# The first block of a two-layer graph network on one Trainium2 core: order of the loads, a second pair of projection banks, and edge chunks turned one ahead

## Chip, cores, metric

The kernel runs on one core of one Trainium2 chip. The metric is the time of one execution on the device in microseconds (us), the median of several runs.

## What is computed

Two layers, each a graph convolution and a feed-forward part, over 6,250 nodes of 256 features and 100,000 edges sorted by destination. The change touches the start of the first convolution, an attention over edges (cut from the reference):

```python
ft = (feat @ W_fc).reshape(N, H, D)              # feat: layer norm of x; H = 8 heads, D = 32
eh = jnp.einsum('nhd,hd->nh', ft, attn_h)
et = jnp.einsum('nhd,hd->nh', ft, attn_t)
fe = (edge_attr @ W_e).reshape(-1, H, D)         # edge_attr: 100,000 x 64
ee = jnp.einsum('ehd,hd->eh', fe, attn_e)
e = jax.nn.leaky_relu(eh[src] + ee + et[dst], negative_slope=NEG_SLOPE)
```

After it come softmax and sum per destination, the first feed-forward part, a second convolution and 32 experts. None of these is changed.

## The kernel before

The program is a row of blocks: `front`, then the attention, the experts of layer 0, the second sums, and the rest. A block ends when all its engines have ended. `front` has five instruction streams written out by hand (SP, POOL, TensorE `pe`, ScalarE `act`, VectorE `dve`); each runs its own in order and meets the others only at semaphores. SP's stream is also the queue of all ordinary transfers.

**Projection.** x (125 partitions x 50 rows, in tile `GX`) comes in ten chunks of five rows (`load_x`, two transfers each). Rows are worked on two at a time, 25 groups: VectorE takes statistics (`stats`), ScalarE the root (`root`), VectorE the reciprocal (`spread`) and normalizes (`norm`); TensorE transposes the group into `pT` (`turn`, L580), ScalarE copies that to `xnT` (`copy_turned`, L655), TensorE multiplies by `Wext`, 272 columns (`project`, L591), ScalarE copies the result from its two PSUM banks `pF` into `row` and `ETS` (`rows`, L665 and L666), and SP stores `row` (`store`, L431). There are two `row` buffers, so the rows of group g wait for the store of group g-2. `project(g)` waits for `row_ready` g, the copies of the group before, since both use `pF`. In ScalarE's order the root of the chunk that group 5 needs stands behind `rows(2)`. Between the projections stand four pieces (`segments`, L572, with `segment_rows` on VectorE) that find where each node's edges begin; the last posts `ROWI` (L740), and POOL then gathers 51 columns of words (L522).

```python
for g in range(NGR):
    if 1 <= g <= len(SW):
        segments(g - 1)
    if g + 1 < NGR:
        turn(g + 1)
    project(g)
```

**Edges.** The edge attributes come in 49 chunks (`load`, three transfers of 512 KB in all, later two) into four buffers `ebuf`; the load of chunk c waits until chunk c-4 is turned. For a chunk TensorE makes eight transposes into `pE0` and `pE1` (`turn_edges`, L553), ScalarE copies both to `eT` (L638), TensorE multiplies by `VB` (`score`, L562, eight products that the profile counts as 16 passes), ScalarE keeps the result in `V` (L644).

```python
for c in range(NCH):
    turn_edges(c)
    ...
    score(c)
```

Into this loop come, at chunk 12, the prefix sum of `TOT` (L617), which VectorE makes from the gathered words (L836), at chunk 13 a second one, and at chunk 24 the turning of the edges' ranks. VectorE works on the ranks meanwhile; SP's queue carries them out and in between the edge loads of chunks 16 to 19 (L471 to L491), and the loads of chunk 19 on are issued behind them.

**POOL** scatters 50 columns of `ETS` (L532) after the words, and then gathers the first 64 columns of projected rows, 128 rows of 264 values each (L540), for the attention.

**End.** Behind the last edge load SP reads `F` (3,136 KB, L497). VectorE makes eight scans over it (L886), adds the scores (L891), SP stores them (L502), and the block ends.

## Time and profile before

| what | us |
|---|---|
| median of 3 runs (3243.67 to 3244.92) | 3244.02 |
| profiled execution, its own time | 3244.61 |
| span of the profile | 3242.9 |
| first block, up to the next one's first instruction | 369.7 |
| TensorE / POOL / VectorE / ScalarE busy over the span | 2347.0 / 1838.9 / 1756.4 / 1314.1 |

Times in the profile count from the start of the span. An engine's idle time stands in brackets ahead of an instruction, with what ended it. A row of the timeline merges neighbours of one kind (x8) and shows the time from the first's start to the last's end, so two merged rows of one engine can overlap by the pipeline's latency; where that matters, starts are compared with starts. "PEclk" is the granted clock of TensorE as a share of full speed (1.00 is 2.4 GHz, 0.50 is 1.2 GHz), "DMA share" the mean busy share of the 16 DMA engines.

### The profile page before, as it was taken

To read this page: it belongs to the slowest core of one execution; us is meant where nothing else is said; L and a number is where in the kernel's file an instruction comes from. 1 tells how busy PE (TensorE), PEld (TensorE's weight loads), DVE (VectorE), ACT (ScalarE), POOL (GpSimd) and SP (SyncE) were. 2 spreads that over 40 slices of the span, in tenths; PEclk is the share of its full clock that TensorE was granted. 3 is DMA by queue.
4 is the path that set the end of the run, shared out by engine and by line. 5 is a ranking of instruction groups with operands and counts; after the bars stand their busy time and mean duration, and the time that the engine had idled before them with its cause. 6 is when DMAs were issued, how large, how long until landed. Compare 5 with 4: busy or idle time off the path is not lost. (4 is left out here: it accounts for less than half of the span.)

```text
span 3242.9 us, 47998 instructions
## 1 busy us (share of the span) xinstructions
PE 2347.0 (72%) x11995; PEld 1955.5 (60%) x11995; DVE 1756.4 (54%) x5705; ACT 1314.1 (41%) x4659; POOL 1838.9 (57%) x1942
## 2 busy tenths in 40 slices
PE   4757476666676665577997888898788988646088
PEld 4656366666666565356776666676666766535077
DVE  5301688888888887466554433333333333366245
ACT  1323355555555444433444433333333332354033
POOL 2674377777777776131000777777777777250645
PEclk9989778888888877688998565655655566757589
DMA  6477444444444446540001333333333333321342
GB/s 194 119 169 202 141 113 112 112 112 113 111 113 112 112 112 156 182 119 23 26 14 43 106 106 106 106 105 105 106 106 106 106 106 105 113 59 28 103 143 85
DMA packets 266022, 349.58 MB, mean 108 GB/s; under 512 B 154605, under 2 KB 195475, under 8 KB 264245
## 3 DMA queue, kind: packets, MB, share of 16 engines
q0 software_dynamic: 89568, 235.89, 25.9%
q1 hardware_dynamic: 176190, 110.72, 13.4%
q8 instruction: 98, 1.61, 0.2%
q14 instruction: 166, 1.36, 0.1%
HBM read 289.49 MB, written 61.20 MB: 108 GB/s over the span
## 5 line engine op out<-in xcount | busy, mean ns | idle before, releaser
L1435 POOL DMA_INDIRECT Gb<-normed_rows,SRCT x784 | 741.2, 945 | 520.4 <-SPq L1427 281.9
L1456 PE MATMUL pAb<-HOTb,Gb 128*128 128x128 f32 x3136 | 843.7, 425 | 151.3 <-DMA Gb<-normed_rows,SRCT 118.1
L1456 PEld LDWEIGHTS pAb<-HOTb,Gb 128*128 128x128 f32 x3136 | 659.6, 297 | 335.5 <-DMA Gb<-normed_rows,SRCT 276.4
L1496 DVE TENSOR_TENSOR ACC<-ACC,pAb 128x256 f32 x784 | 330.7, 422 | 641.8 <-PE pAb L1456 568.6
L1026 POOL DMA_INDIRECT GX<-ft_rows,SRCT x432 | 412.6, 955 | 131.4 <-issue 129.6
L1115 ACT ACTIVATE ACC<-apA 128x254 f32 x784 | 301.0, 384 | 413.9 <-PE apA L1188 340.5
L1188 PE MATMUL apA<-AHOT,GX 128*128 128x129 f32 x1920 | 304.2, 328 | 83.0 <-DVE GX L1337 82.7
L1188 PEld LDWEIGHTS apA<-AHOT,GX 128*128 128x128 f32 x1920 | 289.2, 240 | 101.8 <-DVE GX L1337 101.7
L1475 ACT ACTIVATE HOTb<-OFFb 128x1024 f32<-128x1024 f32 x98 | 103.6, 1057 | 604.8 <-PE pAb L1456 604.6
L1026 POOL DMA_INDIRECT G<-ft_rows,SRCT x288 | 274.5, 953 | 87.6 <-issue 86.4
L1471 ACT ACTIVATE OFFb<-iota,NRELb 128x128 f32<-128x128 f32 x784 | 239.6, 388 | 6.7
L1188 PE MATMUL apA<-AHOT,G 128*128 128x129 f32 x1216 | 198.5, 335 | 48.1 <-DVE G L1337 46.1
L1188 PEld LDWEIGHTS apA<-AHOT,G 128*128 128x128 f32 x1216 | 189.2, 247 | 59.2 <-DVE G L1337 56.8
L1665 POOL DMA_INDIRECT Y<-sums_by_rank,RANKI x50 | 48.4, 968 | 169.9 <-POOLq L152 80.6
L1337 DVE TENSOR_TENSOR GX<-GX,apV 128x1024 f32<-128x1024 f32 x120 | 143.2, 1193 | 0.0
L562 PE MATMUL pS<-VB,eT 128*128 128x128 f32 x784 | 100.8, 283 | 50.3 <-ACT V L644 49.3
L1116 ACT ACTIVATE FL<-apA 128x4 f32<-128x4 f32 x784 | 134.5, 172 | 0.0
L562 PEld LDWEIGHTS pS<-VB,eT 128*128 128x128 f32 x784 | 92.8, 194 | 60.1 <-ACT eT L638 60.1
L2505 POOL DMA_INDIRECT out_dram<-sO,sID x80 | 77.8, 972 | 74.9 <-issue 42.1
L2253 POOL DMA_INDIRECT rows_by_expert<-PAY,POSI x50 | 49.6, 992 | 123.4 <-DVE POSI L2444 108.5
L1992 PE MATMUL fpM<-fxT,ffn_E 128*128 128x250 f32 x400 | 101.2, 407 | 25.2 <-ACT h L1920 25.2
L1237 DVE TENSOR_TENSOR AHOT<-apL,RELT 128x1024 f32<-128x1024 f32 x98 | 118.6, 1210 | 0.0
(390 smaller groups left out, 3968.0 us busy)
## 6 DMA issues: line engine op xcount, KB each, us to landing
ebuf<-in_edge_attr_dram SPq DMA_DIRECT2D x49, 448.0 KB
Gb<-normed_rows,SRCT POOLq DMA_INDIRECT x784, 2.7
rows_by_expert<-ffn_PADT SPq DMA_DIRECT2D x1, 10360.0 KB, 42.2
sT<-rows_by_expert SPq DMA_DIRECT2D x80, 129.5 KB, 2.2
GX<-ft_rows,SRCT POOLq DMA_INDIRECT x480
sums_by_rank<-rrowa SPq DMA_DIRECT2D x49, 128.0 KB, 1.7
sums_by_rank<-rrowb SPq DMA_DIRECT2D x49, 128.0 KB, 1.7
GX<-in_x_dram SPq DMA_DIRECT2D x11, 560.0 KB
```

Source lines behind the costliest of these rows:

```text
L562: last = nc.tensor.matmul(pS[:, m * 2 * H0:m * 2 * H0 + 128], eT[c % 2][:, m * EP:(m + 1) * EP], VB[:, :], start=True, stop=True)
L1026: pool.indirect_dma_start(G[c % GS][:, m, :], None, FT[:, :], bass.IndirectOffsetOnAxis(ap=SRCT[:, t:t + 1], axis=0)).then_inc(g_in[c % GS ...
L1115: nc.scalar.activation(acc[:, :, ds(r + 1, EP - 1)], sums[:, :, 1:EP], ACT.Copy)
L1116: nc.scalar.activation(FL[:, :, f:n + 1:n - f], sums[:, :, 0:HW:EP], ACT.Copy).then_inc(pfree[b], 1)
L1188: last = nc.tensor.matmul(pA[b][:, f * HW:(f + 1) * HW], G[c % GS][:, m, f * 128:(f + 1) * 128], HOT[c % 2][:, m, :], start=True, stop=True)
L1237: nc.vector.tensor_tensor(HOT[c % 2][:, h * HT:(h + 1) * HT, 0:EP], pL[0:EP, 256:256 + EP].unsqueeze(1).to_broadcast([EP, HT, EP]), RELT[: ...
L1337: nc.vector.tensor_tensor(v, v, pV[0:EP, 0:128].rearrange("p (h m) -> p h m", m=UT)[:, :, m:m + WB].rearrange("p h m -> p m h").unsqueeze( ...
L1435: pool.indirect_dma_start(G[g % R][m][:, :], None, TABLE[:, :], bass.IndirectOffsetOnAxis(ap=SRCT[:, t:t + 1], axis=0)).then_inc(g_in[g % ...
L1456: last = nc.tensor.matmul(pA[b][:, o:o + EP], G[k][m][:, c * 128:(c + 1) * 128], HOT[k % 2][:, m, :], start=True, stop=True)
L1471: nc.scalar.activation(OFF[k2][:, m, :], iota[0:EP, 0:EP], ACT.Abs, bias=NREL[k2][:, m:m + 1])
L1475: nc.scalar.activation(HOT[k2][:, :, :], OFF[k2][:, :, :], ACT.Relu, bias=1.0, scale=-1.0).then_inc(hot[k2], 1)
L1496: last = nc.vector.tensor_tensor(acc[:, :, ds(b, EP)], acc[:, :, ds(b, EP)], pA[q][:, o:o + KD * EP].rearrange("p (c r) -> p c r", c=KD), ...
```

## The change

Four things. On SP's queue x comes first: chunk 0 right behind the weights, chunk 1 behind the edge weights, chunks 2 to 9 behind the source indices; the padded destinations (`DXI`) move behind x, then the zeroes, then the four edge chunks; the row stores follow as before. The wait for `idx_set` moves behind chunk 0. The projection of group g uses `pF` for even g and `pE` for odd g (`pN`), and waits for the copies of group g-2. TensorE turns chunk c+1 ahead of the scores of chunk c; before chunk 0 it waits for `row_ready` 24, since `pE` is shared now.

```diff
--- before.py
+++ after.py
@@ -365,6 +365,7 @@
         pT = ps(s, "pT", [128, 512])
         pF = [ps(s, f"pF{m}", [128, 512]) for m in range(GT)]
         pE = [ps(s, f"pE{k}", [128, 512]) for k in range(2)]
+        pN = [pF, pE]
         pS = ps(s, "pS", [128, 512])
         pH = ps(s, "pH", [128, 512])
         pQ = ps(s, "pQ", [128, 512])
@@ -433,33 +434,32 @@
                 sp.dma_start(W[:, :, 0:D], W_fc.rearrange("(k p) n -> p k n", p=128)).then_inc(w_in, 16)
                 sp.dma_start(AH[:, :], attn_h.rearrange("h d -> (h d)").partition_broadcast(128)).then_inc(w_in, 16)
                 sp.dma_start(AT[:, :], attn_t.rearrange("h d -> (h d)").partition_broadcast(128)).then_inc(w_in, 16)
+                load_x(0)
+                ds32 = dst.rearrange("(p j) -> p j", j=BK * BW)
+                for a in PARTS:
+                    sp.dma_start(DVI[a, :], ds32[a, :]).then_inc(dv_in, 16)
                 sp.wait_ge(idx_set, 1)
+                sp.dma_start(SNI[0:P - 1, :], ds32[1:P, 0:1], allow_slow_non_contiguous=True).then_inc(dv_in, 16)
+                for k in range(2):
+                    sp.dma_start(WE[k * DE:(k + 1) * DE, :], W_e[:, :]).then_inc(we_in, 16)
+                sp.dma_start(AE[:, :], attn_e.rearrange("h d -> (h d)").partition_broadcast(128)).then_inc(we_in, 16)
+                load_x(1)
+                sp.dma_start(QI[:, 0:NB, :], src[0:NB * QB * EP].rearrange("(b q p) -> q b p", q=QB, p=EP)).then_inc(q_in, 16)
+                sp.dma_start(QI[0:QL, NB, :], sv).then_inc(q_in, 16)
+                sp.dma_start(QI[QL:QL + 1, NB, 0:E % EP], sl).then_inc(q_in, 16)
+                for q in range(2, NX):
+                    load_x(q)
                 sp.dma_start(DXI[0:112, 1:ES + 1], dv[0:112, :]).then_inc(ld, 16)
                 sp.dma_start(DXI[112:EF, 1:ES + 1], dv[112:EF, :]).then_inc(ld, 16)
                 sp.dma_start(DXI[EF:EP, 1:EL + 1], dl).then_inc(ld, 16)
                 sp.dma_start(DXI[1:EP, 0:1], dv[:, ES - 1:ES], allow_slow_non_contiguous=True).then_inc(ld, 16)
                 sp.dma_start(DXI[0:EF - 1, ES + 1:ES + 2], dv[1:EF, 0:1], allow_slow_non_contiguous=True).then_inc(ld, 16)
                 sp.dma_start(DXI[EF - 1:EF, ES + 1:ES + 2], dl[:, 0:1]).then_inc(ld, 16)
-                load_x(0)
-                ds32 = dst.rearrange("(p j) -> p j", j=BK * BW)
-                for a in PARTS:
-                    sp.dma_start(DVI[a, :], ds32[a, :]).then_inc(dv_in, 16)
-                sp.dma_start(SNI[0:P - 1, :], ds32[1:P, 0:1], allow_slow_non_contiguous=True).then_inc(dv_in, 16)
-                for k in range(2):
-                    sp.dma_start(WE[k * DE:(k + 1) * DE, :], W_e[:, :]).then_inc(we_in, 16)
-                sp.dma_start(AE[:, :], attn_e.rearrange("h d -> (h d)").partition_broadcast(128)).then_inc(we_in, 16)
-                sp.dma_start(QI[:, 0:NB, :], src[0:NB * QB * EP].rearrange("(b q p) -> q b p", q=QB, p=EP)).then_inc(q_in, 16)
-                sp.dma_start(QI[0:QL, NB, :], sv).then_inc(q_in, 16)
-                sp.dma_start(QI[QL:QL + 1, NB, 0:E % EP], sl).then_inc(q_in, 16)
-                load_x(1)
-                for c in range(ER):
-                    load(c)
-                    load_x(2 + c)
                 sp.wait_ge(v_zero, 1)
                 sp.dma_start(STARTD.rearrange("(p j) h -> p (j h)", j=ES), V[:, :]).then_inc(zero_in, 16)
                 sp.dma_start(RSUMD[RB * 128:RB * 128 + 1, :], V[0:1, 0:D]).then_inc(zero_in, 16)
-                for q in range(2 + ER, NX):
-                    load_x(q)
+                for c in range(ER):
+                    load(c)
                 for g in range(NGR):
                     store(g)
 
@@ -583,12 +583,12 @@
 
                 def project(g):
                     pe.wait_ge(xT_ready, g + 1)
-                    if g:
-                        pe.wait_ge(row_ready, g)
+                    if g >= 2:
+                        pe.wait_ge(row_ready, g - 1)
                     for m in range(GT):
                         for c in range(KD):
                             n = m * KD + c
-                            last = nc.tensor.matmul(pF[m][0:P, 0:WX], xnT[g % 2][:, n * P:(n + 1) * P], W[:, c, :],
+                            last = nc.tensor.matmul(pN[g % 2][m][0:P, 0:WX], xnT[g % 2][:, n * P:(n + 1) * P], W[:, c, :],
                                                     start=(c == 0), stop=(c == KD - 1))
                     last.then_inc(f_ready, 1)
 
@@ -610,8 +610,11 @@
                     project(g)
 
                 early, late = 3 * ER, 6 * ER
+                pe.wait_ge(row_ready, NGR - 1)
+                turn_edges(0)
                 for c in range(NCH):
-                    turn_edges(c)
+                    if c + 1 < NCH:
+                        turn_edges(c + 1)
                     if c == early:
                         pe.wait_ge(tot, 1)
                         nc.tensor.matmul(pQ[0:P, 64:65], below[0:P, 0:P], TOT[:, :], start=True, stop=True).then_inc(pre, 1)
@@ -662,8 +665,8 @@
                         act.wait_ge(stored[g % 2], 32 * (g // 2))
                     for m in range(GT):
                         i = g * GT + m
-                        nc.scalar.activation(row[g % 2][:, m, :], pF[m][0:P, 0:D + H0], ACT.Copy)
-                        last = nc.scalar.activation(ETS[0:P, i * H0:(i + 1) * H0], pF[m][0:P, D + H0:WX], ACT.Copy)
+                        nc.scalar.activation(row[g % 2][:, m, :], pN[g % 2][m][0:P, 0:D + H0], ACT.Copy)
+                        last = nc.scalar.activation(ETS[0:P, i * H0:(i + 1) * H0], pN[g % 2][m][0:P, D + H0:WX], ACT.Copy)
                     last.then_inc(row_ready, 1)
 
                 root(0)
```

On SP's queue, ahead of the stores, there stood before (the middle of the queue; names are tiles, `ebuf` an edge chunk, `GX` a chunk of x):

```order
L447 DMA SNI<-in_dst_dram 124x1
L449 DMA eT<-in_L_gnn_W_e_dram 64x256 x2
L450 DMA eT<-in_L_gnn_attn_e_dram 128x256
L451 DMA QI<-in_src_dram 112x6x128
L452 DMA QI<-in_src_dram 109x128
L453 DMA QI<-in_src_dram 1x32
L415 DMA GX<-in_x_dram 112x1280
L415 DMA GX<-in_x_dram 13x1280
L421 DMA ebuf<-in_edge_attr_dram 112x1024
L422 DMA ebuf<-in_edge_attr_dram 15x1024
L424 DMA ebuf<-in_edge_attr_dram 1x1024
L415 DMA GX<-in_x_dram 112x1280
```

Now the last of the queue ahead of the first edge chunk is:

```order
L457 DMA DXI<-in_dst_dram 1x1
L459 DMA et_at_starts<-V 128x6272
L460 DMA sums_by_rank<-V 1x256
L422 DMA ebuf<-in_edge_attr_dram 112x1024
L423 DMA ebuf<-in_edge_attr_dram 15x1024
L425 DMA ebuf<-in_edge_attr_dram 1x1024
```

and behind the fourth edge chunk come the first stores:

```order
L423 DMA ebuf<-in_edge_attr_dram 15x1024
L425 DMA ebuf<-in_edge_attr_dram 1x1024
L432 DMA ft_rows<-row 112x528
L432 DMA ft_rows<-row 13x528
```

All x chunks now lie ahead of `DXI`, zeroes and edges. The same transfers stand ahead of the first row store as before.

On TensorE, from the last two projections into the edge loop, there stood before (in brackets the semaphores that an instruction waits for; `attr_Tcopied` are ScalarE's copies of `pE`, `attr_in` the landed chunk):

```order
L591 MATMUL pF<-Wext,xnT 125x272 [waits row_ready,xT_ready]
L591 MATMUL pF<-Wext,xnT 125x272 x3
L591 MATMUL pF<-Wext,xnT 125x272 [waits row_ready,xT_ready]
L591 MATMUL pF<-Wext,xnT 125x272 x3
L553 MATMUL pE<-ident,ebuf 128x128 [waits attr_in0]
L553 MATMUL pE<-ident,ebuf 128x128 x7
L562 MATMUL pS<-VB,eT 128x128 [waits attr_Tcopied1]
L562 MATMUL pS<-VB,eT 128x128 x7
L553 MATMUL pE<-ident,ebuf 128x128 [waits attr_Tcopied0,attr_in1]
L553 MATMUL pE<-ident,ebuf 128x128 x3
L553 MATMUL pE<-ident,ebuf 128x128 [waits attr_Tcopied1]
L553 MATMUL pE<-ident,ebuf 128x128 x3
```

and now:

```order
L591 MATMUL pE<-Wext,xnT 125x272 [waits row_ready,xT_ready]
L591 MATMUL pE<-Wext,xnT 125x272 x3
L591 MATMUL pF<-Wext,xnT 125x272 [waits row_ready,xT_ready]
L591 MATMUL pF<-Wext,xnT 125x272 x3
L553 MATMUL pE<-ident,ebuf 128x128 [waits attr_in0,row_ready]
L553 MATMUL pE<-ident,ebuf 128x128 x7
L553 MATMUL pE<-ident,ebuf 128x128 [waits attr_Tcopied0,attr_in1]
L553 MATMUL pE<-ident,ebuf 128x128 x3
L553 MATMUL pE<-ident,ebuf 128x128 [waits attr_Tcopied1]
L553 MATMUL pE<-ident,ebuf 128x128 x3
L562 MATMUL pS<-VB,eT 128x128 [waits attr_Tcopied1]
L562 MATMUL pS<-VB,eT 128x128 x7
```

The projections alternate between `pE` and `pF`, the first transposes also wait for `row_ready`, and the transposes of chunk 1 (and so on to the end) stand ahead of the scores of the chunk before.

## Rows read from the trace of the kernel before

**Rows 1.** Timeline, end of the block: start us, us, engine, line, operation, out<-in, count

```profile
331.67 0.36 SPq L497 DMA_DIRECT2D F<-et_at_starts  x1
...
344.20 14.05 DVE L886 TENSOR_TENSOR_SCAN F<-xnT,C,F 128x784 f32<-128x784 f32 x8 [84.24 <-DMA F<-et_at_starts]
...
369.69 0.10 POOL L986 MEMSET HSEL<- 128x8 f32 x1 [75.78 <-POOLq L152]
```

**Rows 2.** Timeline, ScalarE: rows of group 2

```profile
59.57 0.39 ACT L665 ACTIVATE row<-pF 125x264 f32<-125x264 f32 x1 [15.30 <-DMA ft_rows<-row]
```

**Rows 3.** Busy time by stretches: stretch, length, engines, PEclk, DMA share, GB/s

```profile
4.00:20.00 16.00, 0.00 (x0) 0.00 (x0) 5.18 (x22) 0.30 (x1) 6.41 (x5) 1.00 0.77 192
48.00:56.00 8.00, 0.74 (x7) 0.51 (x6) 2.34 (x12) 0.00 (x0) 0.00 (x0) 0.80 1.00 246
60.00:68.00 8.00, 7.48 (x33) 6.54 (x34) 2.98 (x10) 1.85 (x9) 0.00 (x0) 0.60 0.21 66
```

**Rows 4.** Timeline, VectorE and TensorE after the gate

```profile
61.91 0.16 DVE L731 COPY ROWF<-pH 125x13 f32<-125x13 f32 x1
...
64.28 3.82 PE L572 MATMUL pH<-SEG,F 125*125 125x128 f32 x24
67.94 0.59 PE L580 MATMUL pT<-ident,xn 125*128 125x125 f32 x4
68.36 2.00 PE L591 MATMUL pF<-Wext,xnT 128*125 128x272 f32 x8
```

**Rows 5.** Timeline, projection cycle and the last projection

```profile
77.20 0.62 ACT L655 ACTIVATE xnT<-pT 128x500 f32<-128x500 f32 x1
...
77.48 2.07 PE L591 MATMUL pF<-Wext,xnT 128*125 128x272 f32 x8 [0.56 <-ACT ETS L666]
...
79.38 0.59 PE L580 MATMUL pT<-ident,xn 125*128 125x125 f32 x4
...
80.54 2.07 PE L591 MATMUL pF<-Wext,xnT 128*125 128x272 f32 x8 [0.56 <-ACT ETS L666]
...
129.53 2.07 PE L591 MATMUL pF<-Wext,xnT 128*125 128x272 f32 x8 [0.99 <-ACT ETS L666]
```

**Rows 6.** Timeline, one cycle of the edge loop

```profile
190.68 1.04 PE L553 MATMUL pE<-ident,ebuf 128*128 128x128 f32 x8
...
191.38 1.08 ACT L638 ACTIVATE eT<-pE 128x512 f32<-128x512 f32 x2 [2.70 <-PE pE L553]
192.35 0.28 ACT L644 ACTIVATE V<-pS 128x128 f32<-128x128 f32 x1
...
192.78 2.02 PE L562 MATMUL pS<-VB,eT 128*128 128x128 f32 x16 [1.06 <-ACT V L644]
...
194.64 1.04 PE L553 MATMUL pE<-ident,ebuf 128*128 128x128 f32 x8
```

**Rows 7.** Timeline, TensorE: prefix sum at chunk 12, and chunk 19

```profile
179.69 0.28 PE L617 MATMUL pQ<-TOT,below 125*125 125x1 f32 x2
...
225.62 1.97 PE L553 MATMUL pE<-ident,ebuf 128*128 128x128 f32 x8 [18.96 <-DMA ebuf<-in_edge_attr_dram]
```

**Rows 8.** Busy time by stretches, second half of the edge loop

```profile
205.00:222.00 17.00, 1.67 (x15) 1.47 (x14) 0.89 (x5) 0.00 (x0) 12.80 (x14) 0.64 1.02 151
240.00:290.00 50.00, 37.34 (x310) 34.20 (x309) 9.52 (x16) 15.06 (x36) 37.82 (x41) 1.00 0.92 242
305.00:325.00 20.00, 14.70 (x124) 13.67 (x123) 0.00 (x0) 6.28 (x15) 0.00 (x0) 1.00 0.47 134
331.00:345.00 14.00, 10.08 (x84) 9.49 (x85) 0.80 (x1) 4.36 (x11) 0.00 (x0) 1.00 0.71 267
```

**Rows 9.** Timeline, POOL: first and last of the 64 gathers

```profile
214.17 0.99 POOL L540 DMA_INDIRECT GX<-ft_rows,SRCT  x1 [0.30 <-issue]
...
292.96 0.95 POOL L540 DMA_INDIRECT G<-ft_rows,SRCT  x1 [0.30 <-issue]
```

**Rows 10.** Timeline, VectorE: the node totals

```profile
147.21 0.15 DVE L836 COPY TOT<-INC 125x1 f32<-125x1 f32 x1
```

## The prediction, made before the changed kernel ran

> **What bounds the kernel now.** I read the page's slices first, then, since the change touches only the first block, the timeline of that block engine by engine, backwards from its end. The next block begins at 369.7 us of a 3242.9 us span [rows 1]. Ahead of it stands one chain: SP issues the read of `F` at 331.7, once the last edge load is out; VectorE's eight scans wait for it and start at 344.2; from there to the next block it is 25.5 us. So the number to follow is the landing of `F`, 344.2. SP issues the read when chunk 44 is turned (the load of chunk 48, ahead of it, waits for that), so TensorE's walk through 49 edge chunks sets it, and what precedes that walk is the projection.
>
> Four stretches make up the 344.2 us.
>
> *To 59.6.* ScalarE holds back for 15.3 us before the rows of group 2, waiting for the row store of group 0 [rows 2]. Between 48 and 56 us the DMA engines are at 1.00 with TensorE nearly still [rows 3]: on SP's queue the store stands behind all of x, four edge chunks and the zeroes.
>
> *59.6 to 131.4.* After the gate comes a piece at half clock (0.60 granted, the 1.2 GHz level, after the idle time before it), in which the last segment matmuls wait for VectorE's read at 61.9; projection 4 starts at 68.4, 8.8 us after the gate [rows 3, 4]. Then a regular cycle: 77.48 to 80.54 is 3.06 us, and 20 of them lead from 68.36 to 129.53, the last projection, and 1.90 us later the first edge chunk is turned, 131.4 [rows 5]. In each, TensorE stands 0.56 us for the ScalarE copies that empty `pF`.
>
> *131.4 to 225.6.* Transposes start at 190.68, then TensorE waits while ScalarE copies (191.38 on); the scores' 16 passes are issued from 192.78 to 194.64 (1.86 us), where the next chunk's transposes begin: 3.96 us a chunk, all of it one after the other [rows 6]. At chunk 12 TensorE makes the prefix sum, at 179.7. Then the loads that VectorE's ranks need pass through SP, and chunk 19, issued behind them, lands at 225.6 after 19 us of idle TensorE [rows 7].
>
> *225.6 to 344.2.* Again 3.96 us a chunk, but beside 64 gathers of POOL from 214.2 to 293.0 (one per 1.25 us), with the DMA engines at 0.92; without gathers they are at 0.47 [rows 8, 9].
>
> **The change, part by part.**
>
> *x ahead of the edges; DXI behind x.* The queue carries the same transfers ahead of the first store, so it cannot land much sooner; x arriving earlier helps only engines that stand at the gate. What is gained is idle DMA time at the start: share 0.77 over 16 us [rows 3] is 3.7 us unused, because x and the slow small DXI pieces come late. With x issued first I take it all: the gate opens at 55.8, **-3.8**. Bounds: 0 and 3.8 (a loss needs the queue to move fewer bytes per us, for which no row speaks).
>
> *Wait on idx_set behind DVI, and DXI late.* Those memsets are VectorE's first work, and it casts DXI only after all its norms, behind which the transfer is hidden. Nothing; were that cover gone, the cast would wait for some 0.4 MB.
>
> *Two pairs of banks.* Projection 3 now passes before the gate, since it needs only the rows of group 1. After the gate come VectorE's read (2.3 us, 59.57 to 61.91), segments (3.7 to 3.8) and a turn: projection 4 starts 6.9 us after it instead of 8.8, **-1.9** [rows 4]. But TensorE has done 4 us less at half clock by then, so that projection falls in it: 3.8 instead of 2, and its turn, **+2** (bounds 0 and 2). Then the cycle: from projection to turn 1.90, from turn to projection 0.42 (67.94 to 68.36), dense: 2.32 [rows 4, 5]. ScalarE's row copies lie between a projection's end (79.55) and the next one's start (80.54), under 1 us, and the turned copy takes 0.62, so it fits. Where a root and VectorE's norms follow these copies the next turn may come a little late, so I take 2.38: 20 cycles x (3.06 - 2.38) = **-13.6**. What could replace the wait is the store two groups back: it has 2 x 2.38 less the copies' 1 = 3.8 us to be issued and land. No row gives its landing; at the 246 GB/s of 48 to 56 us its 264 KB are 1.1 us of transfer [rows 3], and the present cycle leaves it 2 x 3.06 - 1 = 5.1 us with no wait. Bounds: 0 and -14.8.
> Of a change of this kind the Trainium skill reports, in "TensorE: Matmul & The Clock Gate", under HAM oscillation, that "Adding PSUM double-buffering gave no further gain" to a kernel whose loop had already been made contiguous. By that the 13.6 us are nought; it is the second rival. The row here shows 0.56 us in each cycle in which TensorE waits for nothing but the bank.
>
> The edge loop's first turn moves from 131.4 to 114.1: **-17.3**.
>
> *A chunk turned ahead.* The added wait on row_ready 24 costs nothing: those copies run beside the last projection. In the new order the copies of chunk c+1 (1.1 us) and the keep (0.28) run under the scores of chunk c: 1.86 for 16 passes and half of that for 8 transposes, 2.79 a chunk if fed, at the 2.4 GHz level at which these rows were taken; ScalarE needs half of it [rows 6]. The prefix matmul waits for chunk 13's turn now: 114.1 + 2.4 to turn 1, + 12 x 2.8 + 1 = 151. Its input `TOT` stood ready at 147.2 [rows 10]; it hangs on POOL's word gathers, which follow the gate and come 3.8 + 1.9 earlier, so about 141.6, ready in time. So 179.7 becomes 151, **-11.4** on top, 28.7 in all. From there to the landing of chunk 19 everything is SP, VectorE's ranks and the DMA engines, which keep their 45.9 us: 225.6 becomes 196.9. TensorE just stands longer there.
>
> *The rest becomes a matter of transfers.* Work of the DMA engines, as share times time: an edge chunk 0.47 to 0.50 x 3.95 = 1.9; a gather (0.92 - 0.47) x 1.25 = 0.55; `F`, from 331 to 345, 0.71 x 14 - 1.9 = 8.0 [rows 8]. Left at 196.9: 28 chunks 53 to 54, 64 gathers 35, `F` 8: 97 us. POOL's gathers start at 208.4 (214.2 less 5.8), and in the 12 us before it TensorE, cold and with two pieces to redo, asks for half of what they could move: 6 us lost. At a share of 1.0 `F` lands at 299.9, at the 1.02 of 205 to 222 at 298. I take 299: 118.6 us become 102.1, **-16.5**. Bounds: rivals 1 and 3.
>
> Sum: 17.3 + 11.4 + 16.5 = 45.2. What comes behind `F` (25.5 us) and all later blocks move as they are. The profiled execution took 3244.6 (span 3242.9); less 45.2 is 3199.4. The median of the runs lies 0.6 lower: **3199**.
>
> **Rivals.**
> 1. *Edges get no more than now beside the gathers.* From 208.4 to 288 the chunks stay at 3.95: chunk 22 becomes 42, chunk 44 is turned at 294, `F` lands at 306. 38 us gained, **3206**. For it: 0.92 leaves little. Against: other stretches of this block show 1.00 to 1.02. The Trainium skill, "DMA: Bandwidth & Descriptors", Queues, rings and completion order, says that each engine alternates between the queues that have work, a packet at a time; that would hold the edges to about half.
> 2. *The second pair gives nothing* (the store, or norm, is waited for instead): the loop starts 13.6 later, chunk 19 lands at 210.4, the gathers overlap at once, `F` at 309.5. 34.7 gained, **3209**.
> 3. *The DMA engines carry both.* Then chunks come at 2.79 to the end; chunk 44 is turned at 271, `F` lands 12.5 later. 60.7 gained, **3183**. Against: shares that add to 1.14.
> 4. *Slower.* One mechanism, after chunk 19: in 205 to 222, where the DMA engines stood at 1.02, they moved only 151 GB/s [rows 8]. Should edges asked for this densely beside gathers move no better, then 28 x 0.52 + 64 x 0.135 + 3.2 = 26.4 MB take 175 us, `F` lands at 372: 28 lost, **3272**. It decides below 26.4 MB / 147.3 us = 179 GB/s. Against: edges and gathers together already move 242.
> That sending x first frees the store altogether would need a transfer to overtake those before it; nothing suggests it.
>
> **How the numbers follow.** Forecast 0.62, rivals 0.13, 0.10, 0.11, 0.04. The forecast's own range is 3193 to 3206. To hold eight in ten I go from rival 3 to a little past rival 2: 3183 to 3212. A measurement of this kernel tells about 0.2%, 6.5 us. All but rival 4 are faster by more: 0.96; within 0.2% 0.01; slower 0.03.
>
> **What would show it.** The first row copy after the gate at about 56; projections every 2.3 to 2.4 us and the first edge transpose near 114; edge scores every 2.8 until the idle stretch, which grows from 19 to about 30 us and ends near 197; beside the gathers a DMA share near 1.0, and chunks every 3.4 to 3.6 with TensorE waiting for `ebuf`; `F` landed at about 299; the next block at 325. Wrong would be: a gate still at 59.6, ScalarE waiting for stores in each cycle, or a later block changed in length.

## The result and the profile after

| | before | changed |
|---|---|---|
| median of 4 runs each, us | 3244.47 (3243.67 to 3247.99) | 3196.64 (3193.17 to 3203.93) |
| span of the profiled execution | 3242.9 | 3191.5 |
| next block begins | 369.7 | 323.2 |
| from there to the end of the span | 2873.2 | 2868.3 |

The ratio of the times is 0.9853, with an interval of 0.9835 to 0.9872: 47.8 us faster, 3196.6 against the 3199 forecast. In this profiled execution the first block gave 46.5 us (45.2 forecast); in a second profile of the same kernel, on another chip, it gave 40.4 (next block at 329.3). The 4.9 us that the rest of the first execution is shorter belong to no part of the change (see the section on what was not expected). The total was forecast rightly, and most steps to it; the first step failed: the gate, ScalarE's wait for the row store of group 0 ahead of the rows of group 2, opened later, not earlier.

The timeline of SP's queue in the changed kernel (start us, us, engine, line, operation, out<-in, count):

```profile
10.36 7.52 SPq L449 DMA_DIRECT2D QI<-in_src_dram  x1
17.92 6.57 SPq L416 DMA_DIRECT2D GX<-in_x_dram  x16
...
25.69 0.25 SPq L455 DMA_DIRECT2D DXI<-in_dst_dram  x1
25.99 15.54 SPq L456 DMA_DIRECT2D DXI<-in_dst_dram  x1
...
52.19 1.58 SPq L432 DMA_DIRECT2D ft_rows<-row  x4
```

Two issues take 7.5 and 15.5 us here, where the ones beside them take 0.3: SP stands on them, and the x chunks, then the zeroes and edges, wait behind. Each is the next transfer behind one over an awkward number of partitions (109 in L448, 127 in L455, both prime; they are called the odd pieces below). The first row store is issued at 52.2.

ScalarE's timeline, the gate; it answers to [rows 2]:

```profile
61.40 0.39 ACT L668 ACTIVATE row<-pF 125x264 f32<-125x264 f32 x1 [17.52 <-DMA ft_rows<-row]
```

61.40 instead of 59.57. TensorE's timeline from the gate on; the rows answer to [rows 4 to 7]:

```profile
64.05 5.46 PE L572 MATMUL pH<-SEG,F 125*125 125x128 f32 x24 [13.85 <-DVE ROWF L734]
69.30 0.66 PE L580 MATMUL pT<-ident,xn 125*128 125x125 f32 x4
69.80 2.00 PE L591 MATMUL pF<-Wext,xnT 128*125 128x272 f32 x8
...
77.98 2.00 PE L591 MATMUL pE<-Wext,xnT 128*125 128x272 f32 x8
79.81 0.59 PE L580 MATMUL pT<-ident,xn 125*128 125x125 f32 x4
80.24 2.00 PE L591 MATMUL pF<-Wext,xnT 128*125 128x272 f32 x8
...
116.67 2.00 PE L591 MATMUL pF<-Wext,xnT 128*125 128x272 f32 x8
118.50 1.04 PE L553 MATMUL pE<-ident,ebuf 128*128 128x128 f32 x8
...
131.24 1.04 PE L553 MATMUL pE<-ident,ebuf 128*128 128x128 f32 x8
132.12 1.95 PE L562 MATMUL pS<-VB,eT 128*128 128x128 f32 x16
133.90 1.04 PE L553 MATMUL pE<-ident,ebuf 128*128 128x128 f32 x8
...
153.40 0.28 PE L620 MATMUL pQ<-TOT,below 125*125 125x1 f32 x2
...
197.64 1.97 PE L553 MATMUL pE<-ident,ebuf 128*128 128x128 f32 x8 [27.52 <-DMA ebuf<-in_edge_attr_dram]
...
245.87 1.04 PE L553 MATMUL pE<-ident,ebuf 128*128 128x128 f32 x8
...
249.21 1.09 PE L553 MATMUL pE<-ident,ebuf 128*128 128x128 f32 x8 [0.51 <-DMA ebuf<-in_edge_attr_dram]
...
252.46 1.09 PE L553 MATMUL pE<-ident,ebuf 128*128 128x128 f32 x8 [0.38 <-DMA ebuf<-in_edge_attr_dram]
...
255.76 1.09 PE L553 MATMUL pE<-ident,ebuf 128*128 128x128 f32 x8 [0.42 <-DMA ebuf<-in_edge_attr_dram]
```

This cycle is 2.26 us (77.98 to 80.24) with no wait for a bank; an edge chunk takes 2.66 (131.24 to 133.90) and its row has no idle time ahead of it. The wait for chunk 19 grew from 19.0 to 27.5 us. From 245.87 on TensorE waits for `ebuf` at each chunk: one every 3.3 us (252.46 to 255.76).

Busy time by stretches, changed kernel (columns as in [rows 3, 8]):

```profile
4.00:20.00 16.00, 0.00 (x0) 0.00 (x0) 6.68 (x26) 0.30 (x1) 6.42 (x5) 1.00 0.75 187
...
200.00:220.00 20.00, 19.00 (x156) 18.13 (x155) 2.33 (x12) 8.42 (x19) 15.12 (x17) 0.94 0.70 195
220.00:240.00 20.00, 20.00 (x182) 20.00 (x183) 7.19 (x5) 9.54 (x21) 15.13 (x17) 1.00 0.95 237
240.00:260.00 20.00, 18.27 (x160) 17.51 (x159) 0.00 (x0) 8.64 (x20) 15.13 (x17) 1.00 1.04 263
260.00:280.00 20.00, 17.28 (x147) 16.15 (x146) 0.00 (x0) 8.18 (x19) 15.12 (x17) 1.00 1.04 265
```

The early rate is 187 GB/s, no better than the 192 before. The share reaches 1.04, at 263 to 265 GB/s, only from 240 on; in the 40 us before that TensorE is busy for 19 and 20 of 20 us and the DMA engines are not full. POOL's first gather and the end of the block, on VectorE and POOL (compare [rows 1, 9]):

```profile
216.16 0.99 POOL L540 DMA_INDIRECT GX<-ft_rows,SRCT  x1 [0.30 <-issue]
...
297.68 14.05 DVE L889 TENSOR_TENSOR_SCAN F<-xnT,C,F 128x784 f32<-128x784 f32 x8 [70.29 <-DMA F<-et_at_starts]
...
323.16 0.10 POOL L989 MEMSET HSEL<- 128x8 f32 x1 [27.23 <-POOLq L152]
```

### The profile page after: what moved, and what is told of

It reads as the page before. It is cut to its first block and busy times, and to the rows that moved or that the text cites. A ratio compares the mean times of both kernels' runs of the same rounds, so it can differ in the third digit from the quotient of the medians.

```text
span 3191.5 us, 47998 instructions
## 1 busy us (share of the span) xinstructions
PE 2326.0 (73%) x11995; PEld 1945.7 (61%) x11995; DVE 1756.4 (55%) x5705; ACT 1318.4 (41%) x4659; POOL 1840.9 (58%) x1942
## 3 DMA queue, kind: packets, MB, share of 16 engines
q1 hardware_dynamic: 176190, 110.72, 13.6%
## 5 line engine op out<-in xcount | busy, mean ns | idle before, releaser
L1191 PE MATMUL apA<-AHOT,G 128*128 128x129 f32 x1216 | 191.6, 327 | 52.2 <-DVE G L1340 49.9
L1191 PEld LDWEIGHTS apA<-AHOT,G 128*128 128x128 f32 x1216 | 182.2, 239 | 63.6 <-DVE G L1340 61.0
L1995 PEld LDWEIGHTS fpM<-fxT,ffn_E 128*128 128x128 f32 x400 | 81.9, 207 | 38.6 <-ACT h L1923 27.8
```

The lines of the kernel that those rows point to most:

```text
L1191: last = nc.tensor.matmul(pA[b][:, f * HW:(f + 1) * HW], G[c % GS][:, m, f * 128:(f + 1) * 128], HOT[c % 2][:, m, :], start=True, stop=True)
L1995: last = nc.tensor.matmul(pM[bank[n]][:, 0:GC], w, v, start=(c == 0), stop=(c == len(pairs) - 1))
```

## The experiments

The first four kernels were run on a chip on which every one of them, the kernel before too (3832.29 us), took some 590 us longer; what the traces show of that is told at the end. Ratios there are to the kernel before on that chip, of which there is no profile; the changed kernel was not run there. Up to the first stores, near 60 us, the timelines of that chip are like those of the others.

### The loads alone

The new order of the loads in the kernel before, nothing else:

```diff
-                sp.wait_ge(idx_set, 1)
-                sp.dma_start(DXI[0:112, 1:ES + 1], dv[0:112, :]).then_inc(ld, 16)
...
+                for q in range(2, NX):
+                    load_x(q)
+                sp.dma_start(DXI[0:112, 1:ES + 1], dv[0:112, :]).then_inc(ld, 16)
...
+                for c in range(ER):
+                    load(c)
```

> The kernel before with the new order of loads alone. Theory A (from the changed kernel's trace: the one-column DXI piece, 126 x 1, held SP's queue for 15.5 us behind the x chunks, so the first row store was issued at 52 us and the gate opened at 61.4): gate near 61.4, first edge transpose near 133, time 1 to 3 us above the kernel before. Theory B (the prediction's: the order fills idle DMA time at the start): gate at 55.8, time 3.8 us below it.

Measured: 3837.61 against 3832.29, ratio 1.0015 (1.0004 to 1.0025): this part costs about 5 us (the interval says 1.5 to 9.6). The gate opens at 63.1, the first edge chunk is turned at 189.4. Theory A holds for the gate and for the sign. The column behind which SP is held is over 127 partitions, not the 126 of the expectation. SP's queue:

```profile
25.69 17.72 SPq L455 DMA_DIRECT2D DXI<-in_dst_dram  x1
...
54.07 137.12 SPq L431 DMA_DIRECT2D ft_rows<-row  x50
```

### The second pair of banks alone

```diff
+        pN = [pF, pE]
...
-                    if g:
-                        pe.wait_ge(row_ready, g)
+                    if g >= 2:
+                        pe.wait_ge(row_ready, g - 1)
...
+                pe.wait_ge(row_ready, NGR - 1)
```

> The kernel before with the second pair of banks alone. Theory A: the projection cycle goes from 3.06 to 2.34 us (20 cycles, 14.4 us), projection 4 comes about as early as before; the edge loop keeps 3.96 us a chunk and starts 14 to 16 us earlier, and all of it reaches the end: about 3229. Rival (what the edge loop gains is lost again to the transfers that follow): 3236 or more.

Measured: 3819.56, ratio 0.997 (0.9957 to 0.9982): 12.7 us off (7 to 16), of the 14 to 16 expected. The first edge chunk is turned at 176.2, against 186.4 in the next kernel, which has the same loads and one pair of banks. The banks alone were not run on another chip.

### A chunk ahead alone

```diff
+                turn_edges(0)
                 for c in range(NCH):
-                    turn_edges(c)
+                    if c + 1 < NCH:
+                        turn_edges(c + 1)
```

> The kernel before with the chunk turned ahead alone. Theory A: the first edge transpose stays at 131.4, the prefix matmul comes 13 us earlier than 179.7, chunk 19 lands near 212, and the rest takes 100 us as in the changed kernel instead of 118.6: F lands near 312, 32 us earlier, about 3212. Rival (the ranks or the node totals are waited for when the loop is faster): chunk 19 not before 218, about 3218.

Measured: 3793.61, ratio 0.9899 (0.9883 to 0.9916): 38.7 us off, where 32 were expected.

### Banks and chunk ahead, the loads as before

The changed kernel with SP's order of before:

> The changed kernel with the loads in the order of before. Theory A: gate back at 59.6, DXI pieces issued in 3 us, everything up to the last edge load 2 us earlier: about 3195, 1 to 3 us below the changed kernel. Theory B (x first is worth its 3.8 us): slower than the changed kernel by 2 to 4 us.

Measured: 3781.44, ratio 0.987 (0.9853 to 0.9886): 50.9 us off, where the two parts alone gave 12.7 and 38.7: they add. Whether this kernel is faster than the changed one, as theory A has it, this run does not tell, since the changed kernel was not run on this chip and its ratio elsewhere, 0.9853, lies at the edge of the interval. That the new order of loads costs time rests on the kernel with the loads alone. `DXI` is issued at the start here, and its held issue lasts 3.08 us; the gate opens at 60.9. The sizes of the three parts are those of a chip that is slow from the projections to the middle of the edge loop, so the chunk ahead was repeated on another chip (last experiment).

### The changed kernel once more, beside the next three

> The changed kernel as it is, beside the kernel before on the same chip, since in the runs so far everything ran some 590 us longer (before 3832 us). Where the kernel before takes 3244 us again, this takes 3193 to 3204. Where it takes about 3830, this takes 48 to 52 us less, as the changed kernel with the old order of loads did.

Measured: 3198.2 against 3243.79, ratio 0.9853 (0.9832 to 0.9874). Gate 61.9, held issue 16.3 us, chunk 19 at 198.4, `F` landed 303.9, next block 329.3: between two profiles of one kernel `F` moves by some 6 us, nearly all of it behind chunk 19. Differences of a few us in `F` or in the next block between two single profiles below are no more than that.

### DXI first, then x

As changed, but with `DXI` ahead of the source indices and of all of x but chunk 0:

```diff
                 sp.wait_ge(idx_set, 1)
+                sp.dma_start(DXI[0:112, 1:ES + 1], dv[0:112, :]).then_inc(ld, 16)
+                sp.dma_start(DXI[112:EF, 1:ES + 1], dv[112:EF, :]).then_inc(ld, 16)
...
                     load_x(q)
-                sp.dma_start(DXI[0:112, 1:ES + 1], dv[0:112, :]).then_inc(ld, 16)
```

> The changed kernel with the six DXI transfers back at the start of SP's queue, x, zeroes and edges in the new order. Theory A (the one-column DXI piece stands 15.5 us on SP because it comes behind sixteen x transfers): it is issued in 3 us again, the first store is issued near 35 instead of 52, the gate opens at 57 to 58 instead of 61.4, and the kernel is 3 to 5 us below the changed one. Theory B (the gate is set by the bytes ahead of the store alone): gate and time as in the changed kernel.

Measured: 3198.95, ratio 0.9855 (0.9833 to 0.9877). SP is free of the long wait and issues the first store at 39.2 instead of 52.2, and yet the gate opens at 62.1. Theory A is wrong, B holds for gate and time: when SP gets to the store does not set the gate.

### Odd transfers in two pieces

As changed, with the two pieces that have a prime number of partitions cut at a multiple of 16:

```diff
-                sp.dma_start(QI[0:QL, NB, :], sv).then_inc(q_in, 16)
+                sp.dma_start(QI[0:96, NB, :], sv[0:96, :]).then_inc(q_in, 16)
+                sp.dma_start(QI[96:QL, NB, :], sv[96:QL, :]).then_inc(q_in, 16)
...
-                sp.dma_start(DXI[1:EP, 0:1], dv[:, ES - 1:ES], allow_slow_non_contiguous=True).then_inc(ld, 16)
+                sp.dma_start(DXI[1:113, 0:1], dv[0:112, ES - 1:ES], allow_slow_non_contiguous=True).then_inc(ld, 16)
+                sp.dma_start(DXI[113:EP, 0:1], dv[112:EF, ES - 1:ES], allow_slow_non_contiguous=True).then_inc(ld, 16)
```

> The changed kernel with two transfers cut: the 127-partition DXI column into 112 and 15, the 109-partition part of the source indices into 96 and 13. 
Measured: 3196.35, ratio 0.9853 (0.9831 to 0.9875). SP's queue, and the first stretch:

```profile
10.94 0.40 SPq L449 DMA_DIRECT2D QI<-in_src_dram  x1
11.39 0.25 SPq L450 DMA_DIRECT2D QI<-in_src_dram  x1
...
19.60 0.51 SPq L456 DMA_DIRECT2D DXI<-in_dst_dram  x1
20.16 1.87 SPq L457 DMA_DIRECT2D DXI<-in_dst_dram  x1
```

```profile
4.00:20.00 16.00, 0.00 (x0) 0.00 (x0) 6.93 (x27) 0.30 (x1) 6.42 (x5) 1.00 0.97 234
```

```profile
55.63 0.39 ACT L670 ACTIVATE row<-pF 125x264 f32<-125x264 f32 x1 [14.46 <-DMA ft_rows<-row]
```

The held issues are gone (7.5 and 15.5 us became 0.25 and 1.9), 234 GB/s are moved in the first stretch instead of 187, and the gate opens at 55.6, where the prediction had it (55.8). Everything behind comes 6 to 7 us earlier than in the first profile of the changed kernel: first edge turn 112.0, chunk 19 191.0, `F` 290.8, next block 316.3. Theory A holds, B does not. In the whole kernel's median this gain does not show (3196.35 beside 3198.2): it is the size of the run-to-run spread. Both pieces were cut at once, so their shares in it are not told apart.

That SP is held behind 127 partitions, and not behind 112 and 15, agrees with the Trainium skill, "DMA: Bandwidth & Descriptors", Why a DMA increments its semaphore by 16 and not by 1: a copy is spread over the largest number of DMA engines up to 16 that divides the slowest dimension on both sides, so 127 partitions go through one. No trace here shows which engines a transfer used. That SP then stands on the next issue is what the rows here add.

With this run the gate can be read as a matter of bytes. The same transfers stand ahead of the first store in all these kernels; the faster they are moved between 4 and 55 us, the earlier the gate opens, with one exception of 0.2 us (GB/s by stretch, gate in us):

| kernel | loads | 4 to 20 | 20 to 40 | 40 to 55 | 4 to 55 | gate |
|---|---|---|---|---|---|---|
| odd pieces split | new | 234 | 280 | 321 | 278 | 55.6 |
| chunk ahead alone (repeated) | as before | 198 | 269 | 342 | 268 | 58.2 |
| banks alone | as before | 183 | 263 | 345 | 262 | 59.6 |
| before | as before | 192 | 271 | 323 | 261 | 59.6 |
| chunk ahead alone | as before | 192 | 265 | 327 | 261 | 60.0 |
| banks and chunk ahead | as before | 195 | 258 | 318 | 256 | 60.9 |
| gathers late | new | 190 | 266 | 298 | 252 | 61.0 |
| CONTU in pieces | new | 208 | 250 | 294 | 250 | 61.1 |
| changed | new | 187 | 263 | 297 | 249 | 61.4 |
| DXI first | new, DXI ahead | 156 | 249 | 347 | 249 | 62.1 |
| changed, once more | new | 192 | 254 | 296 | 247 | 61.9 |
| loads alone | new | 195 | 240 | 288 | 240 | 63.1 |

The gate opens at 58.2 to 60.9 in the five profiles with the old order and at 61.0 to 63.1 in the five with the new one. The busy share is the worse measure here: the changed kernel's second profile has 0.87 at 4 to 20 where the first has 0.75, and moves as little (192 and 187 GB/s). The kernel with `DXI` first loses at 4 to 20 what the changed one loses at 40 to 55: SP is held at 8.3 to 13.6 while there is little else in the queue.

### Stores ahead of zeroes and edges

The kernel with `DXI` first, and the zeroes (in four pieces) and first edge chunks sent between the stores:

```diff
-                sp.dma_start(STARTD.rearrange("(p j) h -> p (j h)", j=ES), V[:, :]).then_inc(zero_in, 16)
...
                     store(g)
+                    if g in (3, 5, 7, 9):
+                        a = slice((g - 3) // 2 * ZW, ((g - 3) // 2 + 1) * ZW)
+                        sp.dma_start(sv0[:, a], V[:, a]).then_inc(zero_in, 16)
+                    if g in (11, 13, 15, 17):
+                        load((g - 11) // 2)
```

> As the kernel with DXI first, but the zeroes, cut into four, go behind the stores of groups 3, 5, 7 and 9, and the four edge chunks behind those of groups 11, 13, 15 and 17. Theory A (5.3 MB ahead of the first store make the gate): the gate opens near 40, TensorE does not stand before projection 4, the first edge transpose comes at 100 to 104 instead of 118.5, F lands 14 to 16 us earlier, and the time is 12 to 17 us below the changed kernel. Rival (the row stores now wait in every group, and the loop start moves by less than 6): within 5 us of the changed kernel.

Measured: 3192.79, ratio 0.9845 (0.982 to 0.9871). The gate is gone: the rows of group 2 are copied at 48.01, behind their projection. With the zeroes and edges between the stores ScalarE now waits a little for a store in four places, 1.1 to 1.9 us each. ScalarE's timeline:

```profile
48.01 0.39 ACT L671 ACTIVATE row<-pF 125x264 f32<-125x264 f32 x1 [1.25 <-PE pF L594]
...
75.99 0.39 ACT L671 ACTIVATE row<-pF 125x264 f32<-125x264 f32 x1 [1.56 <-DMA ft_rows<-row]
```

First edge turn 108.2, chunk 19 186.8, `F` 287.0, next block 312.5: 10.7 us earlier than in the first profile of the changed kernel. So what stands ahead of the store in the queue is the gate. The gain is under the 12 to 17 us of theory A, and the first edge turn later than the 100 to 104 expected; in the medians it is 5.4 us (3198.2 to 3192.79), with intervals that overlap.

### Gathers only after the edges

POOL's 64 gathers wait until chunk 44 is turned:

```diff
                 pool.wait_ge(src_ready, 2)
+                pool.wait_ge(e_T[1], NCH - ER)
```

> The changed kernel with POOL's 64 row gathers held until chunk 45 is turned, to see the edge loop without them. Theory A (beside the gathers the DMA engines, at a share of 1.04, set the chunk's time): with them gone a chunk takes 2.66 us to the end, TensorE never waits for ebuf after chunk 19, F is read near 267 instead of 278 and lands near 277 instead of 298. The block then ends with the gathers, near 350, 25 us later than in the changed kernel. Rival (TensorE and ScalarE set the chunk's time, or edges alone fill the engines): F lands not before 292.

One run: 3238.5. POOL gathers from 271.6 on. The windows ahead of that:

```profile
240.00:260.00 20.00, 20.00 (x183) 20.00 (x182) 0.00 (x0) 9.97 (x23) 0.00 (x0) 1.00 0.65 204
```

TensorE is busy for 20.00 of 20 us (18.27 in the changed kernel), an edge chunk takes 2.66 us to the end, the DMA share is 0.65. So it is the gathers' transfers that stretch the chunks to 3.3 us and more. `F` is read only 5.5 us earlier (272.6 for 278.1), since up to 245.9 a chunk takes 2.66 us in the changed kernel too, and lands at 285.6. Both are later than expected (267 and 277), but well ahead of the rival's 292; the gathers, now in the open, push the next block to 363.7.

### The CONTU read in pieces

The one read that stands ahead of the load of chunk 19 on SP is cut in eight, each sent behind an edge chunk:

```diff
-                sp.dma_start(CONTU[:, 0:NCH * EP], CONTP.unsqueeze(0).to_broadcast([H0, UT, NCH * EP])).then_inc(cu_in, 16)
                 for c in range(n + 3, NCH):
                     load(c)
+                    h = c - n - 3
+                    if h < H0:
+                        sp.dma_start(CONTU[h * UT:(h + 1) * UT, 0:NCH * EP], CONTP[:, :]).then_inc(cu_in, 16)
```

> The changed kernel with the 1.57 MB read of CONTU cut into eight, one behind each of the edge loads 19 to 26. Theory A (chunk 19 lands 23 us after the CONTU read because it stands behind it): chunk 19 lands near 178 instead of 197.6, TensorE's idle stretch falls from 27.5 to under 9 us, chunk 44 is turned 15 us or more earlier; the block then ends with POOL's gathers, near 297 to 300 instead of 323: 20 to 26 us below the changed kernel. Rival (the scatters or the rank pieces make the stretch slow, not CONTU): chunk 19 not before 190, gain below 8 us.

Measured: 3194.24, ratio 0.9834 (0.9814 to 0.9854), an interval that overlaps the changed kernel's; the changed kernel was not run on this chip. Rows of TensorE and POOL:

```profile
178.27 1.97 PE L555 MATMUL pE<-ident,ebuf 128*128 128x128 f32 x8 [8.96 <-DMA ebuf<-in_edge_attr_dram]
```

```profile
280.09 0.95 POOL L542 DMA_INDIRECT G<-ft_rows,SRCT  x1 [0.30 <-issue]
281.34 2.34 POOL L542 DMA_INDIRECT G<-ft_rows,SRCT  x1 [0.30 <-issue]
283.98 1.44 POOL L542 DMA_INDIRECT G<-ft_rows,SRCT  x1 [0.30 <-issue]
```

The wait for chunk 19 falls from 27.5 to 9.0 us, and chunk 19 is turned 19.4 us earlier. `F` lands 16.6 earlier (281.1), the next block begins 14.1 earlier (309.0), where 297 to 300 had been expected: the DMA share is at 0.96 to 1.04 from 180 on, so most of the reordered work had to be done anyway, and the last gathers, now beside VectorE's scans (from 281.07), take 1.44 us instead of 0.95 and end at 301, after the scans (295.1).

### All three repairs

Odd pieces split, zeroes and edge chunks between the stores, `CONTU` in pieces; also the rank column of 111 partitions (L488) cut in two:

```diff
-                sp.dma_start(NEXQ[0:QB - 1, :], rq[1:QB, :, 0], allow_slow_non_contiguous=True).then_inc(rq_in, 16)
+                sp.dma_start(NEXQ[0:96, :], rq[1:97, :, 0], allow_slow_non_contiguous=True).then_inc(rq_in, 16)
+                sp.dma_start(NEXQ[96:QB - 1, :], rq[97:QB, :, 0], allow_slow_non_contiguous=True).then_inc(rq_in, 16)
```

> The changed kernel with the odd shapes cut (the 111-partition rank column too), zeroes and edge chunks between the row stores, and CONTU in pieces. Theory A: the gate and the idle stretch both go; first edge transpose near 103, POOL's chain (51 word gathers, 50 scatters, 64 gathers) ends 12 us or more before that of the changed kernel's 295 and sets the end of the block: next block near 285, 35 to 40 us below the changed kernel, near 3160. Rival (one of the three gains hides behind another): not more than 28 us below.

Measured: 3176.3 against 3249.27, ratio 0.9786 (0.977 to 0.9802), the fastest of all; its interval lies below that of the changed kernel. First edge turn at 103.0, chunk 19 at 161.5, `F` at 264.7, next block at 291.6, 31.5 us earlier than in the first profile of the changed kernel. In the block the three gains add (6.9, 10.7 and 14.1 make 31.7). In the time of the whole program, by the ratios, the gain over the changed kernel is 22 us, not the 35 to 40 expected; that is the number of the rival, though not for its reason. Part of the difference is that the rest of the program is 14 us longer in this profile than in that of the changed kernel (see the last section). Of its stretches:

```profile
220.00:240.00 20.00, 17.58 (x153) 16.82 (x153) 0.00 (x0) 8.46 (x19) 15.18 (x16) 1.00 1.04 257
240.00:260.00 20.00, 17.24 (x147) 16.19 (x146) 0.00 (x0) 8.18 (x18) 15.13 (x16) 1.00 1.04 311
```

The DMA share is 1.02 to 1.04 from 200 to 260. Of the 36 us by which chunk 19 came earlier, 33 reach `F`.

### A chunk ahead alone, on another chip

> The kernel before with the chunk turned ahead alone, again, for a chip on which the kernel before takes 3244 us. Theory A: first edge transpose at 131.4, prefix matmul near 166, chunk 19 near 211, F near 311, next block near 337: 31 to 34 us below the kernel before. Rival (what the loop gains is taken by the transfers beside the gathers, which start at the same time as before): 24 us or less below it.

Measured: 3221.18 against 3249.27, ratio 0.9906 (0.9891 to 0.9921), 28 us off; 31 to 34 had been expected, the rival's 24 were passed. Its block ends at 334.6, 35 us earlier than before. Its first edge turn already comes 2.8 us earlier (128.7), which is no work of this change, so 32 us are the chunk ahead's. Chunk 19 is turned at 207.3 after a wait of 27.0 us, `F` lands at 309.1; the DMA share is 1.04 to 1.07 from 220 to 300. So the chunk ahead alone is worth some 32 of the 46.5 us of the block, and already drives the DMA engines to the full.

## Why the prediction was right, and where it was wrong

**Total.** 46.5 us in the block for 45.2; the errors below cancel, and that they do so to 1.3 us is luck, as the second profile of the same kernel shows (changes against the kernel before, us):

| stretch | forecast | changed | once more |
|---|---|---|---|
| to the first edge turn | -17.3 | -12.9 | -12.0 |
| from there to chunk 19 | -11.4 | -15.0 | -15.2 |
| from there to `F` | -16.5 | -18.5 | -13.1 |
| sum | -45.2 | -46.5 | -40.3 |

**x ahead: wrong in sign.** -3.8 forecast, +1.8 measured (59.57 to 61.40), and +5 us for the whole program when made alone. The step that failed is that no row spoke for the queue moving fewer bytes per us, so that a loss was left out of the bounds: between 4 and 55 us it moved 249 GB/s instead of 261. The prediction took the idle DMA time of the start, 3.7 us, for a matter of x and the small `DXI` pieces coming late. Most of it came with the odd pieces, which the change moved but did not remove; behind x, and with SP standing 15.5 us on the next issue, the zeroes and edges were sent late and less was moved at 40 to 55 us instead (297 GB/s for 323). With those pieces split the gate opens at 55.6, 3.9 us before the 59.57 of the kernel before, and 2.5 to 5.3 before the other kernels with the old order. The profile before had shown the two held issues, 3.06 us behind a `DXI` column and 3.31 behind 109 partitions of `QI`. SP's timeline of the kernel before:

```profile
5.30 0.25 SPq L440 DMA_DIRECT2D DXI<-in_dst_dram  x1
5.59 3.06 SPq L441 DMA_DIRECT2D DXI<-in_dst_dram  x1
...
13.74 3.31 SPq L453 DMA_DIRECT2D QI<-in_src_dram  x1
```

The prediction named "slow small DXI pieces" and did not price what happens when they are issued behind x.

**From gate to projection 4: size right, place off.** 8.4 us (61.40 to 69.80) against 8.8 before; the forecast was 6.9, and 2 more that half clock would cost in projection 4, 8.9 in all. The half clock (0.51 granted from 64.0 to 69.5) fell on the segment matmuls (5.46 us for 3.8), not on projection 4, which ran at 1.00: TensorE now stands idle for 13.85 us right ahead of the segments.

**Cycle: right.** 46.87 us for 20 (69.80 to 116.67), 2.34 each; forecast 2.38, before 3.06. ScalarE waits for a store once more, 1.3 us at 110.5, and the average holds all the same. Rival 2 fell with it. The first edge turn came at 118.5: 12.9 us earlier, where 17.3 were forecast; the gate, 5.6 us later than forecast (61.4 for 55.8), is more than the difference. What the Trainium skill reports of another kernel, "Adding PSUM double-buffering gave no further gain" ("TensorE: Matmul & The Clock Gate", HAM oscillation), did not carry over to this one: 0.56 us of bank wait a cycle went, and the banks alone were worth 12.7 us.

**Edge chunk: a little too dear.** 2.66 us, forecast 2.79. The 1.86 and 1.86/2 of [rows 6] were taken where TensorE had stood before each piece; run back to back the scores take 1.78 (132.12 to 133.90) and the transposes 0.88. So the prefix sum follows 34.9 us after the first turn (36.9 forecast) and stands at 153.4 (151 forecast).

**Chunk 19: right.** 197.6 for 196.9, with 27.5 us of idle TensorE ("about 30"). From the prefix sum to it there are 44.2 us, 1.7 fewer than the 45.9 taken over from before; with the 2.4 us of delay at the prefix sum that comes to 0.7.

**POOL's chain: wrong.** Forecast 5.8 us earlier, it came 2.0 later: the gathers begin at 216.2 (214.5 in the second profile), not 208.4, and `TOT` was ready at 148.4, not 141.6. The chain follows the gate, and its first word gather stands at 71.7 (70.3 before). The prefix sum, at 153.4, did not have to wait for it. In the kernel with the odd pieces split the gathers do begin at 209.2.

**Rest: the sum right, the place of the limit not.** 100.0 us to `F` for 102.1, and 105.4 in the second profile. The mean DMA share from 197.6 to 297.7 is 0.94, so 94 us of work for the 97 reckoned. But the engines do not set the pace from the gathers' start on: until 245.9 TensorE turns a chunk every 2.66 us (save 5.1 at its restart and one stretch of 5.9) and waits for none, and only from there does one come every 3.0 to 3.7 us, at a share of 1.04 where 1.0 to 1.02 was reckoned. Rival 1 (edges held at 3.95 beside the gathers) fell: chunk 44 was turned at 275.9, not 294. Rival 3 fell on the share: with the gathers away, chunks do come at 2.66. Rival 4 fell: 263 GB/s, not under 179. What is open is why edges and gathers together reach 263 GB/s at a share of 1.04 and the stretch with `F` 325 at 0.98; the runs do not tell.

## What to carry to other kernels

Read the queue's own timeline before a transfer is moved: an issue that takes 3 us instead of 0.3 belongs to the transfer ahead of it, and the 3 us become 15 when more is in flight; cut such a transfer at a multiple of 16 partitions. What a wait for a store costs is set by the bytes that stand ahead of it in its queue, so send what is needed late behind it. When a compute loop is made denser, add up the DMA work that is left, as share times time: here that sum (97 us at a share of 1, some 94 measured) gave the landing of `F` to 1.3 us in one profile and 4.9 in the other.

## What was not expected of the hardware

**One issue held for 3 to 18 us.** The same transfer, a column of 4-byte elements over 127 partitions, held the next issue for 3.1 us at the start (before), 5.3 behind chunk 0 of x, and 15.5 to 17.7 behind all of x; the piece over 109 partitions did so for 3 to 7.5, the column over 111 (no prime number) for 4.7 (169.87), and for 0.8 once it was cut in two.

**Gathers beside VectorE's scans** took 1.44 us instead of 0.95, in three kernels (gathers late, `CONTU` in pieces, all three repairs). Why was not tried.

**A chip on which other engines stand while POOL issues indirect DMAs.** On the chip of the first four kernels TensorE waited, once for 42.8 us, with "issue" as the reason while POOL scattered and gathered. TensorE's timeline of the kernel with banks and chunk ahead there:

```profile
219.70 1.11 PE L554 MATMUL pE<-ident,ebuf 128*128 128x128 f32 x4 [9.25 <-issue]
263.57 3.76 PE L563 MATMUL pS<-VB,eT 128*128 128x128 f32 x16 [42.76 <-issue]
275.15 1.09 PE L554 MATMUL pE<-ident,ebuf 128*128 128x128 f32 x4 [7.82 <-issue]
```

and its DMA queues in 205 to 300 us:

```profile
q0 software_dynamic: 3045, 5.57, 22.5%
q1 hardware_dynamic: 320, 1.05, 3.8%
q14 instruction: 1, 0.01, 0.0%
```

One packet on the instruction queues in 95 us, where the kernel before on the other chip has six. Once POOL is done the loop runs at full speed again (TensorE 40.00 of 40 us busy from 440 to 480). What makes the engines stand is open; no run tested it. The ratios of one change agree on both chips all the same (the chunk ahead: 0.9899 and 0.9906).

**The rest of the program** takes 2868 to 2886 us in ten profiles of the nine kernels of the ordinary chips, which have the same code there. In three of them (`DXI` first, all three repairs, the chunk ahead repeated), with 2881 to 2886, the median of POOL's 784 gathers in the second sums is 949 ns, in the others 946; this is 2.4 us over that stretch; where the remainder lies was not followed. Differences under some 10 us between two of these kernels are therefore read from the block, not from the total, and those under 6 not from `F` or the block's end either, but from the gate and the first edge turn.
